# A layer of experts, attention and experts: constant products on TensorE and a new order of work in the routing stage

## The chip, the cores and the metric

The kernel runs on one core of one Trainium2 chip. The metric is the device time of one execution in microseconds (us): the median of the runs, and beside it one execution that the hardware profiler recorded. A core has five engines that run side by side and meet at semaphores: TensorE (PE: matrix products; PEld is its loading of weights), VectorE (DVE), ScalarE (ACT), GpSimd (POOL) and SyncE (SP), whose queue issues most DMAs.

## The reference

The input x is 2 x 2048 tokens of width 256, so 4096 tokens. Three layers follow each other, each with a layer norm before it and a residual sum behind it:

```
x = x + 0.5 * ffn(layernorm(x))     # router: 8 experts, the best 2 of each token; silu(gate) * up, down
x = x + attention(layernorm(x))     # causal convolution to q, k, v of width 64; 8 heads; blocks of 128 tokens
x = x + 0.5 * ffn(layernorm(x))     # the same experts again
```

In an ffn, `logits = h @ router_w.T`; the two largest probabilities of a token, normalised to sum 1, weigh the outputs of their experts (hidden width 176).

## The kernel before

Tokens lie in 32 tiles of 128. An expert layer doesn't run all experts on all tokens: it sorts the 8192 pairs of token and expert by expert into slots, in 71 tiles of 128 slots, gathers the rows of each slot tile, runs the one expert of that tile, and adds the two results of each token later. So three stages are long and regular: the experts of the first layer (from about 82 us to 231 us of the span), the attention with the routing of the last layer, and the experts of the last layer. The change touches the first stage, which ends when the first expert tile can start at about 82 us: it normalises all 32 tiles, computes router logits, finds each token's two experts and slots, and splits the experts' weights in two.

Every engine runs one list of instructions in a fixed, hand-written order. A wait at the head of a list holds all that is behind it. In the first stage the lists are:

- **SP**: loads of x in 8 chunks, then the experts' weights, then the stores of normalised rows of tile groups 0 and 1 (`stored0`, `stored1`), 13 small loads for the attention, then the stores of groups 2 and 3. A group is 8 tiles.
- **GpSimd**: a few constants, the correction of the reciprocal roots of two parts of the tiles (`correct_roots`, one Newton step in small operations), 16 or so further constants (`other_constants`), the roots of the other three parts, a first indirect DMA to warm up (`warm_up`, which it waits for), and then the gathers of rows (L655), which wait for the token table `tok_i`.
- **ScalarE**: logarithm and exponential for the roots (`seed`), the normalisation of tile t + 4 (`norm`, L866), the copy of the turned tile t out of PSUM (L882), and in the turns 22, 25, 28 and 30 the high parts of the weights of experts 0 to 3 (`weights`, L872). After the loop it evicts what TensorE makes of the low parts (`lows`, L894), with the high parts of experts 4 to 7 between, and some weights of the attention. Last comes an exponential (`difference`) and the load of the table for silu (L748).
- **TensorE**: in each turn of `first_router` two transposes of a tile (L1447) and the logits of the tile before (L1454: two f32 products of 8 columns, that the trace shows as four). `first_ranks(g)` (L1471 to L1477) counts, for a group, how many earlier tokens chose each expert. `low_parts(e)` (L1507, L1508) subtracts the high part of an expert's weights from the whole in PSUM, in three pieces; `first_counts` gives the totals; `first_table(g)` (L1491) turns the slots of a group into the table of tokens, from the lanes and the tile marks of the group.
- **VectorE**: means and variances (`first_stats`), `constants`, and for each group g: `first_pick(g)` (L1002 to L1017: the two experts), `first_places(g)` (L1026 to L1035: the slots, after the ranks), `first_lanes(g)` (L1041: 16 operations of 128x128 that mark the lane of each slot). After all groups come `first_starts` (L1055 to L1063), the tile marks `first_tiles` (L1048), the lanes of group 3, the low part of the last expert (`low_part`, L1068), the token table `tok_i` (L1105), and a few products for the attention and the weights of the sums.

The lanes of groups 2 and 3 lie over the buffer that holds the normalised rows of group 2 (the tensor `yg`), so VectorE waits for `stored2` before it writes the first of them. The order of the end is this:

```python
for g in range(GROUPS - 1):
    first_tiles(g)
first_lanes(3, 0, GROUP)
first_tiles(3)
...
for e in range(PE_LOW, E):
    low_part(e)
v.wait_ge(first["table"], 1)
```

Of the kernel before, what the change touches and what calls it, by code (L numbers as in the profile page):

```python
# [15 lines left out]
ALU = mybir.AluOpType  # L16
# [4 lines left out]
BF16 = mybir.dt.bfloat16  # L21
# [3 lines left out]
P = 128  # L25
# [4 lines left out]
E, TOPK = 8, 2  # L30
# [20 lines left out]
PROJB_AT = 5  # L51
HEAD_AT = [4 * (h % 2) + h // 2 for h in range(NH)]
GROUP = 8
GROUPS = TILES // GROUP
STATS = ((0, 4), (4, 4), (8, 8), (16, 8), (24, 8))
# [6 lines left out]
WEIGHTS_AFTER = {22: 0, 25: 1, 28: 2, 30: 3}  # L62
PE_LOW = 7
# [33 lines left out]
def macaron_kernel(nc, x, conv_w, conv_b, wq, wk, wvT, wo, bq, bk, bo, proj_w, proj_b, gupT, dpT, rwT,  # L97
                   out, h_dram, y_dram):
    ctx = ExitStack()
    with ctx:  # L100
# [149 lines left out]
        def lane_num(j):  # L250
            return lane_halves[j // TILES][:, j % TILES, :]
# [25 lines left out]
        mask_4 = mask_bf[:, :].unsqueeze(1).to_broadcast([P, 4, P])  # L277

# [299 lines left out]
        def _(pool):  # L578
# [127 lines left out]

            stats_of = list(enumerate(STATS))
            correct_roots(stats_of[0:2])
            other_constants()
            correct_roots(stats_of[2:])  # L710
            warm_up()
            gather_rows(0)
# [7 lines left out]
        def _(a):  # L720
# [42 lines left out]
            def attention():  # L763
# [77 lines left out]
                a.wait_ge(projb, 4)  # L841
# [11 lines left out]
            def first_norm():  # L853
# [26 lines left out]
                for t in range(TILES):  # L880
                    a.wait_ge(first["transposed"], t + 1)
                    a.activation(hT_sb[:, t % 2, :], (A, B)[t % 2][:, 0:D], ACT.Copy).then_inc(first["copied"], 1)  # L882
                    if t in SEED_AFTER:
                        seed(SEED_AFTER[t])
                    if there(t + LEAD):
                        norm(t + LEAD)
                    if t in WEIGHTS_AFTER:
                        weights(WEIGHTS_AFTER[t])

# [6 lines left out]
                for e in range(4):  # L896
                    lows(e)
                    weights(e + 4)
                a.wait_ge(loaded, 16 * len(loads))
                attention_weights()  # L900
                for e in range(4, PE_LOW):
                    lows(e)
# [29 lines left out]
        def _(v):  # L932
# [137 lines left out]
            def first_layer():  # L1070
                r = R[0]
                for c in range(4):
                    first_stats(c)
                constants()
                for c in range(4, len(STATS)):
                    first_stats(c)
                first_pick(0)
                first_places(0)
                first_pick(1)
                first_lanes(0, 0, GROUP)  # L1080
                first_places(1)
                first_lanes(1, 0, GROUP)
# [6 lines left out]
                v.tensor_tensor(wtmp[:, 1, :], best[:, :, 1], best[:, :, 0], ALU.subtract).then_inc(r["diff"], 1)  # L1089
                first_lanes(2, GROUP // 2, GROUP)  # L1090
                first_places(3)
# [10 lines left out]
                for e in range(PE_LOW, E):  # L1102
                    low_part(e)
# [3 lines left out]
                v.wait_ge(first["turned"], 1)  # L1107
                v.tensor_scalar(at_i[:, 0:TABLE_TILES], CC[0:1, EXPERTS_AT:EXPERTS_AT + TABLE_TILES], float(EW), None,
                                ALU.mult).then_inc(r["weights_at"], 1)
                v.wait_ge(wprep, 5)  # L1110
# [298 lines left out]
        def _(pe):  # L1409
# [29 lines left out]

            def first_router():  # L1440
                z = first

                def turn(t):
                    pe.wait_ge(z["normed"], t + 1)
                    pe.wait_ge(z["copied"], t + 1)
                    for c in range(DC):
                        i = pe.transpose((A, B)[t % 2][:, c * P:(c + 1) * P],  # L1447
                                         h_rings[t // GROUP][:, t % GROUP, c * P:(c + 1) * P], ident[:, :])
                    i.then_inc(z["transposed"], 1)

# [35 lines left out]
            def first_table(g):  # L1486
                n = GROUP * TOPK
                pe.wait_ge(first["lanes"], g + 1)
# [236 lines left out]

            pe.wait_ge(rw_in, 16)
# [5 lines left out]
            first_ranks(GROUPS - 1)  # L1732
            low_parts(2)
            first_counts()
            low_parts(3)
            pe.wait_ge(loaded, 16 * len(loads))
            weights_vo()
            low_parts(4)
# [3 lines left out]
            low_parts(5)  # L1742
            first_table(GROUPS - 1)
            turn_experts()
            low_parts(6)
# [5 lines left out]
            pe.wait_ge(projb, 3)  # L1751
            pe.wait_ge(qk_scaled, 2)
            pe.wait_ge(const, 5)
# [50 lines left out]
```

## Time and profile before

| | |
|---|---|
| median of 3 runs | 793.61 us (789.54 to 793.93) |
| the profiled execution's own time | 796.36 us |
| its span, first to last instruction | 794.6 us |
| busy in the span | PE 690.0, PEld 603.7, DVE 528.2, ACT 490.2, POOL 335.8 us |
| mean granted TensorE clock | 0.961 |

The span is that of the one profiled execution; 1.8 us of its own time lie around the span, and it is 2.7 us above the median of the runs. Times in rows of the timeline count from the start of the span. A row of the timeline is: start, duration, engine (with q for its queue of issued DMAs), line, operation, what it writes and reads, shapes, and in brackets the idle time before it and what ended that. xN merges N neighbours of the same kind, so the duration is that of all of them.

### The profile page before, as it was taken

How to read it: one execution, taken by the hardware profiler on the slowest of the kernel's cores; microseconds unless marked ns; L12 is line 12 of the kernel's file. 1: busy time of each engine (PE TensorE's matmuls, PEld its weight loads, DVE VectorE, ACT ScalarE, POOL GpSimd, SP SyncE). 2: the span in 40 equal slices, each digit the busy share in tenths (PEclk: the TensorE clock that was granted, in tenths of full speed). 3: DMA queues.
4: the chain of work that ended last, by engine and by line, in shares of the span. 5: the costliest groups of instructions: out<-in, count | busy, mean ns of one | idle time of the engine just before them, and what ended most of it. 6: DMA issues, size and time to landing. Idle time of an engine off the chain costs nothing. (4 is left out here: it accounts for less than half of the span.)

```text
span 794.6 us, 19426 instructions
## 1 busy us (share of the span) xinstructions
PE 690.0 (87%) x5468; PEld 603.7 (76%) x5468; DVE 528.2 (66%) x1813; ACT 490.2 (62%) x1734; POOL 335.8 (42%) x361
## 2 busy tenths in 40 slices
PE   3999799999999799998988889989635999999944
PEld 3976699999975688877767777778424999999833
DVE  6578566666656587786767576857664777777643
ACT  4766566666653587767766657767522666666633
POOL 5100544444416444455555545252551444444500
PEclk9999999999999999999999999999956999999979
DMA  9930354444422110011111111010124444444279
GB/s 313 279 110 13 124 147 141 143 130 127 128 82 85 39 41 28 28 41 55 55 55 48 61 41 48 22 55 2 61 91 117 132 128 125 128 131 126 83 288 346
DMA packets 57863, 83.40 MB, mean 105 GB/s; under 512 B 9520, under 2 KB 43827, under 8 KB 57780
## 3 DMA queue, kind: packets, MB, share of 16 engines
q1 hardware_dynamic: 44772, 47.63, 19.0%
q0 software_dynamic: 13008, 34.69, 14.0%
q8 instruction: 49, 0.80, 0.4%
q14 instruction: 34, 0.28, 0.1%
HBM read 45.77 MB, written 37.44 MB: 105 GB/s over the span
## 5 line engine op out<-in xcount | busy, mean ns | idle before, releaser
L1539 PE MATMUL CC<-w_hi,turned_parts 128*128 x568 | 172.5, 345 | 0.3 <-DVE turned_parts L1161 0.2
L655 POOL DMA_INDIRECT shared<-h_rows,tok_i x71 | 67.3, 948 | 119.0 <-issue 58.7
L667 POOL DMA_INDIRECT y_rows<-shared,y_dest x71 | 69.9, 985 | 88.7 <-DVE y_dest L1173 74.9
L683 POOL TENSOR_TENSOR pr<-pr,prec 128x1024 f32<-128x1024 f32 x31 | 58.8, 1895 | 112.2 <-DVE prec L1353 110.9
L1539 PEld LDWEIGHTS CC<-w_hi,turned_parts 128*128 128x128 f32 x568 | 103.8, 190 | 1.0 <-issue 0.9
L1539 PE MATMUL CC<-w_lo,turned_parts 128*128 x284 | 91.8, 323 | 0.0
L729 ACT ACTIVATE shared<-CC 128x176 f32<-128x176 f32 x142 | 45.1, 317 | 75.1 <-PE CC L1539 72.6
L813 ACT ACTIVATE pr<-SS,nmax 128x128 f32<-128x128 f32 x256 | 90.4, 400 | 0.8 <-issue 0.8
L700 POOL DMA_INDIRECT h_regions<-h_store,dest x64 | 63.1, 987 | 47.3 <-DVE dest L1256 27.3
L1156 DVE TENSOR_TENSOR shared<-shared,CC 128x176 f32<-128x176 f32 x142 | 48.0, 338 | 51.6 <-ACT shared L729 30.0
L691 POOL DMA_INDIRECT yg<-y_rows,slot_i x64 | 62.6, 977 | 34.9 <-DMA y_rows<-shared 15.5
L745 ACT ACTIVATE shared<-SS 128x256 f32<-128x256 f32 x142 | 54.6, 385 | 26.5 <-issue 15.5
L804 ACT ACTIVATE shared<-CC 128x512 f32<-128x512 f32 x64 | 34.7, 594 | 48.1 <-PE CC L1629 45.2
L813 ACT ACTIVATION_READ_ACCUMULATOR pr<-SS,nmax 128x1 f32 x256 | 61.8, 241 | 0.0
L1539 PEld LDWEIGHTS CC<-w_lo,turned_parts 128*128 128x128 f32 x284 | 54.1, 191 | 0.0
L1556 PE MATMUL SS<-w_hi,turned_parts 128*128 x142 | 51.8, 364 | 1.3 <-DVE turned_parts L1167 1.0
L1161 DVE TENSOR_TENSOR turned_parts<-A,turned_parts 128x256 fp32r<-128x256 f32 x72 | 30.6, 425 | 29.5 <-ACT turned_parts L734 28.5
L1311 DVE TENSOR_REDUCE nmax<-SS 128x8 f32<-128x1024 f32 x32 | 39.1, 1221 | 13.4 <-PE SS L1623 10.4
L1623 PEld LDWEIGHTS SS<-shared 64*128 64x128 f32 x512 | 31.1, 187 | 18.0 <-issue 9.7
L1161 DVE TENSOR_TENSOR turned_parts<-B,turned_parts 128x256 fp32r<-128x256 f32 x70 | 29.8, 425 | 21.0 <-ACT turned_parts L734 16.8
L1526 PE MATMUL A<-ident,shared 128*128 128x128 f32 x144 | 29.0, 283 | 16.1 <-DMA shared<-h_regions 12.6
L781 ACT ACTIVATE lnvar<-moments,eps 128x2 f32<-128x2 f32 x39 | 11.7, 300 | 48.9 <-DVE moments L1367 48.0
(318 smaller groups left out, 2055.4 us busy)
## 6 DMA issues: line engine op xcount, KB each, us to landing
shared<-h_regions SPq DMA_DIRECT2D x71, 129.0 KB
y_rows<-shared SPq DMA_DIRECT2D x71, 128.0 KB
w_lo<-y_rows SPq DMA_DIRECT2D x9, 512.0 KB, 8.4
x_sb<-in_x_dram SPq DMA_DIRECT2D x8, 512.0 KB, 8.3
out_dram<-x_sb SPq DMA_DIRECT2D x16, 256.0 KB, 5.7
w_hi<-y_rows SPq DMA_DIRECT2D x7, 512.0 KB, 11.9
w_lo<-in_gupT_dram SPq DMA_DIRECT2D x2, 1408.0 KB, 10.7
h_regions<-pad_rows SPq DMA_DIRECT2D x15, 129.0 KB
```

The source lines that it names most:

```text
L655: pool.indirect_dma_start(out=rows[:, s % RING, 0:D], out_offset=None, in_=h_dram[:, :], in_offset=bass.IndirectOffsetOnAxis(ap=tok_i[:, s ...
L667: pool.indirect_dma_start(out=y_dram[0:TOPK * TOKENS, :], out_offset=bass.IndirectOffsetOnAxis(ap=y_dest[:, s:s + 1], axis=0), in_=y_sb[:, ...
L683: pool.tensor_tensor(pr[:, q, :, :], pr[:, q, :, :], prec[:, q, :].unsqueeze(2).to_broadcast([P, NH, P]), ALU.mult).then_inc(t["norm"], 1)
L691: pool.indirect_dma_start(out=yg[:, q, k, :], out_offset=None, in_=y_dram[:, :], in_offset=bass.IndirectOffsetOnAxis(ap=slot_i[:, b, k:k + ...
L700: pool.indirect_dma_start(out=h_regions[:, :], out_offset=bass.IndirectOffsetOnAxis(ap=dest[:, q, k:k + 1], axis=0), in_=hr[:, q, :], in_o ...
L729: a.activation(gate[:, p, :], CC[:, 512 * p:512 * p + H], ACT.Silu).then_inc(r["silu"], 1)
L745: a.activation(y_sb[:, u % RING, :], SS[:, 512 * (u % 2):512 * (u % 2) + D], ACT.Copy).then_inc(r["y_sb"], 1)
L813: e = a.activation(pr[:, u % 2, h, :], SS[:, h * P:(h + 1) * P], ACT.Exp, bias=nmax[:, u % 2, h:h + 1], accum_out=psums[:, u % 2, h:h + 1])
L1156: v.tensor_tensor(hid[:, p, 0:H], gate[:, p, :], CC[:, 512 * p + H:512 * p + GU], ALU.mult).then_inc(r["hid"], 1)
L1161: v.tensor_tensor(rowsT_lo[:, p, :], (A, B)[p][:, 0:D], rowsT_hi[:, p, :].bitcast(F32), ALU.subtract).then_inc(r["rowsT_lo"], 1)
L1539: i = pe.matmul(CC[:, 512 * (u % 2):512 * (u % 2) + GU], rows_part[:, u % 2, c * P:(c + 1) * P], weights, start=(n == 1), stop=(n == 3 * DC))
L1556: pe.matmul(acc, hidA_hi[:, u % 2, :], w_hi[:, at_a], start=True, stop=False)
```

## The change

All edits lie in the first stage.

- **Constant products.** VectorE clears a bf16 tile of 128x128 (`idle_bf`, over the buffer `rank4`, which is free then) as its first instruction. TensorE waits for it and then runs 28 products of 512 columns with it into PSUM bank CC, before it waits for the router weights. After the two transposes of every turn it runs one more such product. Nothing reads the results.
- **Roots and statistics.** VectorE makes all five parts of the statistics before `constants`. GpSimd corrects the roots of three parts, not two, before its further constants.
- **Lanes.** GpSimd makes the lanes of groups 0 and 1, 16 operations each, after its warm-up DMA and before it waits for the stores and `tok_i`; VectorE tells it on the semaphore `const` when the places of a group are there. VectorE keeps groups 2 and 3.
- **Order on VectorE.** The second half of the lanes of group 2 comes after `first_places(3)` instead of before. One more expert's low part is VectorE's (`PE_LOW` is 6, not 7: TensorE and ScalarE make experts 0 to 5, VectorE 6 and 7), and both come after `tok_i` instead of before.
- **Order on ScalarE.** No weights in the turns; after the loop `weights(0)`, `weights(1)`, and then for e of 0 to 5 `lows(e)` and `weights(e + 2)`, with the attention's weights after e = 2.
- **Order on TensorE.** `first_counts` follows the ranks of group 3 at once; the attention's products come after `low_parts(2)`, and each later piece of the list is one `low_parts` earlier.

```diff
-PROJB_AT = 5
+PROJB_AT = 6
...
-WEIGHTS_AFTER = {22: 0, 25: 1, 28: 2, 30: 3}
-PE_LOW = 7
+PE_LOW = 6
...
+        idle_bf = rank4[:, :, :, :].rearrange("p i k e -> p (i k e)").bitcast(BF16)
...
+            def first_lanes(g):
+
+                pool.wait_ge(const, 5 + g)
+                for b in range(g * GROUP, (g + 1) * GROUP):
+                    for k in range(TOPK):
+                        ins = pool.tensor_scalar(lane_num(TOPK * b + k), iota_h[:, :], slane[:, b, k:k + 1],
+                                                 number_off[:, b:b + 1], ALU.is_equal, ALU.mult)
+                ins.then_inc(first["turned"], 1)
+
             stats_of = list(enumerate(STATS))
-            correct_roots(stats_of[0:2])
+            correct_roots(stats_of[0:3])
             other_constants()
-            correct_roots(stats_of[2:])
+            correct_roots(stats_of[3:])
             warm_up()
+            first_lanes(0)
+            first_lanes(1)
             gather_rows(0)
...
-                    if t in WEIGHTS_AFTER:
-                        weights(WEIGHTS_AFTER[t])
...
-                for e in range(4):
+                weights(0)
+                weights(1)
+                for e in range(PE_LOW):
                     lows(e)
-                    weights(e + 4)
-                a.wait_ge(loaded, 16 * len(loads))
-                attention_weights()
-                for e in range(4, PE_LOW):
-                    lows(e)
+                    weights(e + 2)
+                    if e == 2:
+                        a.wait_ge(loaded, 16 * len(loads))
+                        attention_weights()
...
-                for c in range(4):
+                v.memset(idle_bf[:, :], 0.0).then_inc(projb, 1)
+                for c in range(len(STATS)):
                     first_stats(c)
                 constants()
-                for c in range(4, len(STATS)):
-                    first_stats(c)
                 first_pick(0)
                 first_places(0)
+                v.sem_inc(const, 1)
                 first_pick(1)
-                first_lanes(0, 0, GROUP)
                 first_places(1)
-                first_lanes(1, 0, GROUP)
+                v.sem_inc(const, 1)
...
+                first_places(3)
                 first_lanes(2, GROUP // 2, GROUP)
-                first_places(3)
                 first_starts()
...
-                for e in range(PE_LOW, E):
-                    low_part(e)
                 v.wait_ge(first["table"], 1)
...
-                v.wait_ge(first["turned"], 1)
+                v.wait_ge(first["turned"], 3)
...
+                for e in range(PE_LOW, E):
+                    low_part(e)
                 v.wait_ge(wprep, 5)
...
+            def busy_clock(n):
+
+                for _ in range(n):
+                    pe.matmul(CC[:, 0:512], idle_bf[:, :], idle_bf[:, :].unsqueeze(1).to_broadcast([P, 4, P]),
+                              start=True, stop=True, skip_group_check=True)
+
...
                     i.then_inc(z["transposed"], 1)
+                    busy_clock(1)
...
-                pe.wait_ge(first["lanes"], g + 1)
+                if g < 2:
+                    pe.wait_ge(first["turned"], g + 1)
+                else:
+                    pe.wait_ge(first["lanes"], g - 1)
...
+            pe.wait_ge(projb, 1)
+            busy_clock(28)
             pe.wait_ge(rw_in, 16)
             pe.wait_ge(made, 3)
             first_router()
...
             first_ranks(GROUPS - 1)
+            first_counts()
             low_parts(2)
-            first_counts()
-            low_parts(3)
             pe.wait_ge(loaded, 16 * len(loads))
             weights_vo()
-            low_parts(4)
+            low_parts(3)
             bias_vo()
             for g in range(GROUPS - 1):
                 first_table(g)
-            low_parts(5)
+            low_parts(4)
             first_table(GROUPS - 1)
             turn_experts()
-            low_parts(6)
+            low_parts(5)
```

The remaining edits shift counts of the semaphores `projb` and `const` by what is added to them.

## Rows read from the trace of the kernel before

**Rows 1.** Timeline of GpSimd (POOL) in the first stage.

```profile
13.95 0.29 POOL L599 CAST ident_bf<-ident 128x128 bf16<-128x128 f32 x1
...
31.97 1.19 POOL L639 DMA_INDIRECT shared<-in_x_dram,part_i  x1 [0.17 <-issue]
...
78.01 0.97 POOL L655 DMA_INDIRECT shared<-h_rows,tok_i  x1 [44.85 <-DVE tok_i L1105]
```

**Rows 2.** Timeline of TensorE (PE) in the first stage.

```profile
16.01 0.67 PE L1447 MATMUL A<-ident,h_store 128*128 128x128 f32 x2
...
24.03 0.67 PE L1447 MATMUL A<-ident,pr 128*128 128x128 f32 x2
...
25.21 0.67 PE L1447 MATMUL B<-ident,pr 128*128 128x128 f32 x2
...
52.53 1.95 PE L1507 MATMUL A<-w_lo,ident 128*128 128x480 f32 x2
...
57.63 1.04 PE L1507 MATMUL B<-w_lo,ident 128*128 128x480 f32 x2
...
60.50 0.20 PE L1471 MATMUL CC<-sel_bf,before_bf 128*128 128x64 bf16 x1
...
75.95 0.69 PE L1491 MATMUL CC<-tile_oh,yg 128*128 128x72 f16 x16
...
81.54 0.44 PE L1526 MATMUL A<-ident,shared 128*128 128x128 f32 x2 [1.89 <-DMA shared<-h_rows,tok_i]
```

**Rows 3.** Timeline of ScalarE (ACT) in the first stage.

```profile
25.91 0.38 ACT L882 ACTIVATE hT_sb<-B 128x256 f32<-128x256 f32 x1 [0.30 <-PE B L1447]
...
58.04 1.30 ACT L872 ACTIVATE w_hi<-w_lo 128x960 fp32r<-128x960 f32 x2
...
80.20 1.28 ACT L748 ACT_TABLE_LOAD   x1
```

**Rows 4.** Timeline of VectorE (DVE) in the first stage.

```profile
31.72 0.27 DVE L1026 TENSOR_REDUCE group_sum<-sel_bf 128x8 f32<-128x64 bf16 x1 [5.48 <-PE CC L1477]
...
36.73 3.66 DVE L1041 TENSOR_SCALAR shared<-iota_h,slane,number_off 128x128 f16<-128x128 f16 x16 [0.15 <-DVE sel_bf L1017]
...
63.73 0.17 DVE L1055 COPY ecnt<-CC 128x8 f32<-128x8 f32 x1 [1.19 <-PE CC L1483]
...
66.61 3.90 DVE L1048 TENSOR_TENSOR tile_oh<-iota_h,stile_h 128x1152 f16<-128x1152 f16 x3 [0.18 <-DVE stile_h L1063]
...
73.99 1.35 DVE L1048 TENSOR_TENSOR tile_oh<-iota_h,stile_h 128x1152 f16<-128x1152 f16 x1
...
75.59 1.48 DVE L1068 TENSOR_TENSOR w_lo<-w_lo,w_hi 128x960 fp32r<-128x960 f32 x2
76.99 0.22 DVE L1105 TENSOR_SCALAR tok_i<-CC 128x72 int32<-128x72 f32 x1
...
77.27 0.67 DVE L1111 TENSOR_TENSOR wvo_lo<-SS,wvo_hi 128x512 fp32r<-128x512 f32 x1
...
80.22 0.18 DVE L1119 TENSOR_SCALAR wtmp<-wtmp 128x32 f32<-128x32 f32 x1 [2.08 <-ACT wtmp L919]
...
82.50 0.42 DVE L1161 TENSOR_TENSOR turned_parts<-A,turned_parts 128x256 fp32r<-128x256 f32 x1 [0.75 <-ACT turned_parts L734]
```

**Rows 5.** Timeline of the queue of SyncE: the store of group 2.

```profile
40.12 0.40 SPq L498 DMA_DIRECT2D h_rows<-yg  x1
```

**Rows 6.** DMA issues of the first 84 us: name, count, size, median us to landing.

```profile
h_rows<-yg SPq DMA_DIRECT2D x1, 1024.0 KB, 4.4
```

**Rows 7.** Timeline of TensorE: constant products ahead of the attention.

```profile
233.02 9.67 PE L1581 MATMUL F<-mask_bf,ident_bf 128*128 128x512 bf16 x44
```

**Rows 8.** Windows of 5 us: busy time of each engine, granted clock (PEclk), DMA share, GB/s.

```profile
20.00:25.00 5.00, 5.00 (x28) 5.00 (x28) 2.77 (x23) 4.00 (x12) 1.26 (x6) 1.00 1.08 289
...
85.00:90.00 5.00, 2.80 (x19) 2.25 (x19) 1.99 (x8) 1.54 (x7) 2.14 (x3) 1.00 0.22 64
...
260.00:265.00 5.00, 2.48 (x8) 2.22 (x9) 3.01 (x7) 3.30 (x18) 0.94 (x1) 0.71 0.18 54
265.00:270.00 5.00, 4.74 (x42) 3.91 (x41) 4.10 (x10) 1.47 (x4) 3.84 (x3) 0.94 0.11 31
```

More of the change, by code:

```diff
@@ L840, in attention @@
                 a.activation(projb_all[:, D:], zeros[:, 0:G_USED - D], ACT.Copy)
-                a.wait_ge(projb, 4)
+                a.wait_ge(projb, 5)
                 a.activation(projb_all[:, 0:D], G[:, 0:D], ACT.Copy).then_inc(projb, 1)
@@ L1750, in _ @@
             experts(R[0])
-            pe.wait_ge(projb, 3)
+            pe.wait_ge(projb, 4)
             pe.wait_ge(qk_scaled, 2)
-            pe.wait_ge(const, 5)
+            pe.wait_ge(const, 7)
             pe.matmul(G[:, 0:D], ones_r[:, :], projb_parts[:, :], start=True, stop=True).then_inc(projb, 1)
```

## Prediction

> **What bounds the kernel now.** All edits lie ahead of the first expert tile, so I first looked for what decides when that tile starts, in the timelines of the engines, from the end backwards. TensorE turns the first gathered rows at 81.54 us, after waiting for their DMA [rows 2]. GpSimd issued that gather at 78.01, after 44.85 us of waiting for `tok_i` [rows 1]. VectorE wrote `tok_i` at 76.99, and ahead of it worked without a pause: tile marks, lanes, tile marks, a low part [rows 4]. So VectorE's list behind the router loop sets the start. ScalarE comes close: its table load ends at 81.48 [rows 3], just as the rows arrive. The start of that list is set by the loop on TensorE: a turn takes 1.18 us (24.03 to 25.21), the loop ends at 52.53 where `low_parts` begins [rows 2], and ScalarE waits for TensorE inside it (0.30 us before a copy) [rows 3].
>
> The reader should also see at which clock the loop runs. The granted clock of 20 to 25 us reads 1.00 [rows 8], but the rows of the work say the lower level (1.2 GHz): the same pair of f32 products of 480 columns takes 1.95 us at 52.53 and 1.04 us at 57.63 [rows 2]. I take the column to be empty ahead of its first event. TensorE rose behind five us of dense products, and the loop before, of transposes and products of 8 columns, had not raised it.
>
> Everything behind the start (experts, attention, experts) is untouched. I take it to shift as a whole, so the result is the move of that start.
>
> **The loop.** Removed from ScalarE's turns: the high parts of four experts, 1.2 us each without the overlap of the rows' 1.30 [rows 3]; they move behind the loop, where ScalarE otherwise waits for TensorE. Added: one product of 512 columns per turn. At the upper level (2.4 GHz) it takes 9.67 / 44 = 0.22 us [rows 7], at the lower twice that, 0.44. If the clock is high, a turn is half of 1.18 plus 0.22 = 0.81 us; some latencies don't halve, so 0.81 to 0.86. If it is low, 1.18 + 0.44 = 1.62, or 1.45 where weight loads hide under the product. Turn 4 starts at 16.01 before [rows 2]; up to there the loop hangs on the first roots, which don't move, so I place it at 15.1 with fast transposes. The third part of the roots comes ahead of GpSimd's constants, so turns 5 to 10, which took 8.0 us instead of 6 x 1.18 = 7.1 (16.01 to 24.03) [rows 2], no longer pause. GpSimd's constants move behind it, and VectorE's first pick waits for them until about 21.5 us; its ranks are wanted after turn 15, so that is covered. With 27 turns of 0.83 (22.4), three rank groups and two pairs of seeds (1.5), and 0.5 for a wait on the picks of group 1, turn 31 runs at 39.5 to 40.1. The ranks and places of group 2 then end at about 42.3.
>
> **The 28 products.** They start at about 1.1 us, run at the lower level first, and end between 9 and 10.5, by when in the run the clock rises. Turn 0 hangs on the first roots until about 9.8, and ScalarE can't copy its result until about 11.4. So they cost nothing, up to about 1 us more than the cover.
>
> **VectorE's list.** Its next wait is `stored2`: SP issued that store at 40.12 behind 13 loads [rows 5], and it took 4.4 us to land [rows 6], so 44.5. The loads themselves are behind x and the weights, where the DMA engines are full, so an earlier `stored1` frees at most 1.5 us: 43.0 to 44.5, and I take 43.5. This new wait hides about 1 us of the loop. From there the rows of before can be added: half the lanes of group 2, 1.8; pick and places of group 3, 5.0 (31.72 to 36.73, the same pair for other groups); the other half, 1.8; starts, 2.9 (63.73 to 66.61); three tile marks, 3.9; lanes of group 3, 3.6; last marks, 1.3 [rows 4]. That is 20.3, so the marks end at 63.8. TensorE has been waiting, and its table of group 3 takes 0.7 [rows 2]; `tok_i` starts at 65.0, not 76.99. That is 12.0 us earlier. Of these the loop gives about 8 to 9, the 32 lanes that leave VectorE 2 x 3.66 (partly in waits before), and the low part of 1.5 behind `tok_i` the last piece.
>
> **What is late next.** Two low parts are now behind `tok_i`, and the last high part is behind `lows(5)`. TensorE starts `low_parts(5)` behind the table, at 65.0, and takes 2.9 us (57.63 to 60.50) [rows 2]: 67.9. ScalarE evicts (0.4) and makes the high part of expert 7, 1.2 [rows 3]: 69.5. VectorE's second piece of its low part ends at 70.5, `wvo_lo` adds 0.7 [rows 4], and TensorE may start at about 71.3. ScalarE, with exponential and table load 1.3 [rows 3], is ready at 70.9. The rows landed at 65.9 + 3.5 = 69.4 (78.01 to 81.54 before). VectorE still has the weights of the sums (from 80.22 to its first low rows at 82.50 it took 2.3, with 0.75 of waiting, so 1.5) and starts its first expert work at 73.0, not 82.50 [rows 4]. The move of the start is 9.5 us: 2.5 of the 12.0 go to this tail.
>
> **Lanes on GpSimd.** No row has this operation there. The nearest is a cast of 128x128 at 0.29 us [rows 1]; I take 0.35, with 0.25 and 0.8 as bounds. GpSimd is free after its warm-up DMA, which was issued at 31.97 [rows 1] and comes some 5 us earlier; it waits for the landing, so the lanes start at about 33.5 and end at 44.7, or 59.1 at 0.8. They are wanted at about 59.2, with the tile marks of group 2. So the price can be anything up to 0.8 at no cost; from there each 0.1 adds 3.2 us. Behind them on GpSimd stand only the gathers, which wait for `tok_i` anyway. For the two engines in each other's way I add 0.5 us. The sum is -9.0 us: 787.4 on the profiled execution's own 796.36, and 784.6 on the median, which is 2.7 below it. Less than nothing isn't excluded for the lanes: VectorE may gain from a calmer list, but `stored2` caps it, at 1 us.
>
> **Rival 1: the clock stays low, slower.** Between turn 0 and turn 4 TensorE waits for roots and copies, and does little. In a stretch without any work the clock fell (0.71 in 260 to 265) and came back only with dense products (0.94 in the next) [rows 8]. If it falls there and one product of 512 columns a turn can't raise it, turns take 1.45 to 1.62 instead of 0.83: turn 31 runs at 56 to 60, VectorE's list starts 14 to 18 us later than 43.5, and the sum is +5 to +9: 801 us. For it speaks the old loop, which never rose; against it that with gaps and 2.8 busy us of 5 the clock stayed up from 85 to 90 [rows 8], and that a product of 512 columns is a large part of a turn. The point of decision is whether the loop runs high from about turn 6 on. The Trainium skill ("TensorE: Matmul & The Clock Gate", Part 4) says that transposes don't count as work for the clock in the way products do. By that rule the transposes of the loop help nothing and the constant products must carry it alone; the old loop agrees, but no row here tells its share of products from its share of transposes. A fall that is made good by turn 6 or 8 costs 0 to 3 us, of which `stored2` hides 1.
>
> **Rival 2: GpSimd and VectorE block each other.** If each of VectorE's operations that meets a lane waits for it, and each lane for one of VectorE's (0.25), a lane takes 0.6 and the lanes end at 52.7. From 43.5 to 52.7 some 15 operations of VectorE wait 0.35 each: +5, so 790 us. In the rows of before, small operations of GpSimd ran beside statistics without a visible delay, but that is one input on VectorE. The Trainium skill ("SBUF — State Buffer", section "SBUF: two separate sides") states such an exclusive lock on a shared pair of ports, for two-input and fast modes of VectorE. It is a rule against this change, and no row of before has such a pair side by side.
>
> **Rival 3: the wait is only moved.** If `stored2` lands no earlier than 44.5 and the tail is 1 us longer (last high part), the sum is -7: 786.6.
>
> **How the numbers follow.** One per cent is 7.9 us, about what a measurement of this kernel can tell from no change. The forecast (high clock, -7 to -11.5) has 0.55, with its own range of 782 to 787; rival 1 has 0.2, rival 2 0.1, rival 3 or a late return of the clock 0.1, and other things 0.05. Faster by over 1% needs at least -7.9: three quarters of the forecast's cases, and some larger gains, 0.5. Slower by over 1% is half of rival 1 and some others, 0.14. The rest, 0.36, is within 1%. The range runs from 780.5, with `stored2` at 43.0 and no conflict, to 800.5, which takes in rivals 2 and 3 and the better edge of rival 1.
>
> **What would show it.** Pairs of transposes in the loop start 0.8 to 0.9 us apart (else 1.45 to 1.6); turn 31 near 40; a wait of VectorE for the store before its first lanes; `tok_i` near 65.0; lanes on GpSimd of 0.35 us; the first low rows at about 73.0. The prediction is wrong if the clock is low in the loop, if a lane costs over 0.8, or if the last weights hold the experts longer than 2.5 us.

## The result, and the profile after

The changed kernel took 801.73 us (median of 4 runs, 799.1 to 803.79), the kernel before 792.25 in the same comparison: a ratio of 1.0118, with an interval of 1.0085 to 1.0151. It is slower by 9.5 us, where I forecast 784.6 us, 9.0 less than the median on record then. What happened is rival 1: the clock falls in the head and stays low through the loop.

The windows of the changed kernel show it first. The column after POOL is the granted clock; the row of 20 to 25 us answers to the first of [rows 8].

```profile
5.00:10.00 5.00, 3.77 (x18) 1.51 (x16) 4.69 (x21) 1.26 (x4) 1.86 (x9) 1.00 1.06 347
10.00:15.00 5.00, 2.91 (x17) 2.08 (x18) 4.71 (x23) 3.68 (x11) 1.44 (x7) 0.94 1.11 351
15.00:20.00 5.00, 5.00 (x23) 4.54 (x24) 3.78 (x24) 3.36 (x9) 3.36 (x17) 0.50 1.04 381
20.00:25.00 5.00, 5.00 (x23) 4.54 (x23) 1.34 (x11) 2.98 (x8) 0.97 (x6) 0.50 1.09 269
...
60.00:65.00 5.00, 5.00 (x26) 3.92 (x27) 1.99 (x10) 2.78 (x5) 5.00 (x8) 0.50 0.00 0
```

The 28 products bring the clock up (they take 7.71 us below, 0.28 each, where the lower level would give 0.44); between 10 and 15 us TensorE has 2.91 us of work, and from 14.37 us on the granted clock is 0.50, that is 1.2 GHz, until 68.98. The row of 15 to 20 us is the instructive one: TensorE is shown busy for all of it, and so it is in the turns behind it, and yet the clock is not granted again. The timeline of TensorE (start, duration, line, operation) shows the two levels of the clock and the path to the first expert tile:

```profile
1.06 7.71 PE L1453 MATMUL CC<-rank 128*128 128x512 bf16 x28 [1.06 <-DVE rank L1083]
...
12.80 0.38 PE L1453 MATMUL CC<-rank 128*128 128x512 bf16 x1
14.24 0.94 PE L1471 MATMUL F<-rw_sb,hT_sb 128*128 128x8 f32 x4 [1.06 <-ACT hT_sb L894]
15.04 0.67 PE L1463 MATMUL B<-ident,h_store 128*128 128x128 f32 x2
15.49 0.63 PE L1453 MATMUL CC<-rank 128*128 128x512 bf16 x1
...
60.45 0.67 PE L1463 MATMUL B<-ident,tile_oh 128*128 128x128 f32 x2
...
63.21 1.95 PE L1527 MATMUL A<-w_lo,ident 128*128 128x480 f32 x2
...
87.39 0.68 PE L1511 MATMUL CC<-tile_oh,yg 128*128 128x72 f16 x16 [1.48 <-DVE tile_oh L1059]
...
95.32 0.41 PE L1546 MATMUL A<-ident,shared 128*128 128x128 f32 x2 [4.24 <-DVE mha_bias L1122]
```

The product at 12.80 takes 0.38 us, the one at 15.49 takes 0.63; the transposes go from 0.41 to 0.67, which is what they took before [rows 2]. Turns are now 1.60 us apart, against 1.18 before: the added product costs its full 0.42 us in each. Turn 31 runs at 60.45, and the first expert's rows are turned at 95.32, not at 81.54 [rows 2]. VectorE and GpSimd answer to [rows 4] and [rows 1]:

```profile
62.69 0.27 DVE L1037 TENSOR_REDUCE group_sum<-sel_bf 128x8 f32<-128x64 bf16 x1 [8.44 <-PE CC L1494]
...
88.11 0.23 DVE L1113 TENSOR_SCALAR tok_i<-CC 128x72 int32<-128x72 f32 x1 [0.55 <-PE CC L1511]
...
92.43 1.53 DVE L1079 TENSOR_TENSOR w_lo<-w_lo,w_hi 128x960 fp32r<-128x960 f32 x2 [2.48 <-ACT w_hi L884]
...
96.26 0.42 DVE L1171 TENSOR_TENSOR turned_parts<-A,turned_parts 128x256 fp32r<-128x256 f32 x1
```

```profile
40.48 25.23 POOL L713 TENSOR_SCALAR shared<-iota_h,slane,number_off 128x128 f16<-128x128 f16 x32 [3.39 <-DMA shared<-in_x_dram,part_i]
...
89.15 1.72 POOL L656 DMA_INDIRECT shared<-h_rows,tok_i  x1 [23.45 <-DVE tok_i L1113]
```

VectorE waits 8.44 us for the ranks of group 2, so the loop, not VectorE's list, holds the start. A lane table on GpSimd takes 25.23 / 32 = 0.79 us, not 0.35, but ends at 65.7, before anyone wants it. From `tok_i` (88.11) to TensorE's first rows (95.32) it is 7.2 us instead of 4.6: the wait ends on `mha_bias`, behind the last low part, behind ScalarE's last high part.

### The profile page after: what moved, and what is told of

Its sections match the earlier page's. It is cut to its first block, busy times and chain, and to the rows that moved or that the text cites. A ratio compares the mean times of both kernels' runs of the same rounds, so it can differ in the third digit from the quotient of the medians.

```text
span 801.7 us, 19528 instructions
## 1 busy us (share of the span) xinstructions
PE 703.1 (88%) x5519; PEld 611.1 (76%) x5519; DVE 524.0 (65%) x1784; ACT 491.7 (61%) x1731; POOL 362.0 (45%) x393
## 3 DMA queue, kind: packets, MB, share of 16 engines
q0 software_dynamic: 13008, 34.69, 13.8%
## 4 chain that ended last, share of the span: by engine, by line
PE 77%; issue 7%; DVE 6%; DMA 4%; ACT 3%; SPq 2%; another core or an unknown queue 1%; POOL 1%; DVEq 0%; POOLq 0%; ACTq 0%
PE CC L1559 17%; PE CC L1709 4%; PE SS L1643 4%; PE CC L1649 4%; PE B L1622 4%; PE F L1699 4%; PE F L1719 3%; PE B L1631 3%; PE A L1546 3%; PE SS L1576 2%; PE SS L1577 2%; PE SS L1578 2%; PE SS L1579 2%; PE SS L1580 2%; PE B L1546 2%
## 5 line engine op out<-in xcount | busy, mean ns | idle before, releaser
L701 POOL DMA_INDIRECT h_regions<-h_store,dest x64 | 63.5, 992 | 43.4 <-issue 21.9
L1576 PE MATMUL SS<-w_hi,turned_parts 128*128 x142 | 51.7, 364 | 1.0 <-DVE turned_parts L1177 0.7
```

Of the source, the lines that this page charges most:

```text
L701: pool.indirect_dma_start(out=h_regions[:, :], out_offset=bass.IndirectOffsetOnAxis(ap=dest[:, q, k:k + 1], axis=0), in_=hr[:, q, :], in_o ...
L1576: pe.matmul(acc, hidA_hi[:, u % 2, :], w_hi[:, at_a], start=True, stop=False)
```

## The experiments

All ratios are to the kernel before on the same chip in the same comparison. The chips differ: the kernel before took 757.9 us (median of 19) beside e1 to e4, 792.7 (27) beside e5 to e8, 758.8 (20) beside e9 to e12. So only ratios and the times of the first stage are compared across groups; for the changed kernel, the one that was profiled on two chips, its start agrees within 1.4 us. "Start" is the time at which TensorE turns the first gathered rows; it was 81.54 before [rows 2].

**e1: the changed kernel without any constant product.**

```diff
-                    busy_clock(1)
...
-            busy_clock(28)
```

> The changed kernel without any constant product (neither the 28 nor the one per turn); all else as changed. Theory A (the clock falls between turn 1 and turn 4, and one product of 512 columns a turn costs 0.43 us at the lower level and doesn't raise it again): turns start 1.18 us apart instead of 1.60, turn 31 at about 49 instead of 60.45, the first expert tile about 11.5 us earlier than in the changed kernel, time about 790 us. Theory B (the lanes on GpSimd, 0.79 us each instead of 0.35, and their clash with VectorE are what costs): the time stays near 800. Theory C (the tail behind tok_i, 7.2 us from tok_i to the first expert tile instead of 4.5, is the whole loss): then at least 799, since the tail is unchanged here.

Measured: 759.03 us (10 runs), ratio 1.0020, interval 1.0005 to 1.0035. The loop and the work behind it, on TensorE:

```profile
47.62 0.67 PE L1463 MATMUL A<-ident,tile_oh 128*128 128x128 f32 x2
...
48.79 0.67 PE L1463 MATMUL B<-ident,tile_oh 128*128 128x128 f32 x2
...
83.42 0.41 PE L1545 MATMUL A<-ident,shared 128*128 128x128 f32 x2 [4.24 <-DVE mha_bias L1122]
```

Turns are back at 1.17 us, and nearly all of the loss is gone: the products cost it. But the rest of the change isn't worth the 3 us or so that was expected of it. The loop ends 1.4 us earlier than before (48.79 against 50.19), `tok_i` comes 0.8 earlier (76.21 against 76.99), and the longer tail, 7.2 us, takes more than that back: the start is 1.9 us later. With 32 lanes off VectorE its last marks still end at 75.34, as before (73.99 + 1.35 [rows 4]): those lanes lay in waits for the loop.

**e2: the changed kernel with more products in turns 1 to 5, where the head was sparse.**

```diff
+HEAD_FILL = {1: 5, 2: 6, 3: 2, 4: 2, 5: 2}
...
-                    busy_clock(1)
+                    busy_clock(HEAD_FILL.get(t, 1))
```

> The changed kernel with more constant products in the sparse head of the loop: 5 after turn 1, 6 after turn 2, 2 after each of turns 3 to 5, and one after all others as now; they fill waits of TensorE. Theory A: the clock doesn't fall at 14 us, stays at 2.4 GHz through the loop with one product a turn, turns start 0.83 to 0.86 us apart, turn 31 at about 40, tok_i near 65 to 66, the first expert tile near 72 to 73, time 780 to 784 us. The lanes then end at about 59, just when the table wants them, and may cost up to 2 us more. Rival D (one product a turn can't hold the clock either): the clock falls later in the loop, turns go back to 1.60, time 790 to 803.

Measured: 754.29 us (10 runs), ratio 0.9955, interval 0.9929 to 0.9980. TensorE, then VectorE and GpSimd:

```profile
14.16 0.61 PE L1472 MATMUL F<-rw_sb,hT_sb 128*128 128x8 f32 x4
14.63 0.42 PE L1464 MATMUL B<-ident,h_store 128*128 128x128 f32 x2
...
20.26 0.42 PE L1464 MATMUL B<-ident,pr 128*128 128x128 f32 x2
...
63.92 0.69 PE L1512 MATMUL CC<-tile_oh,shared 128*128 128x72 f16 x16 [2.02 <-POOL shared L714]
64.45 0.69 PE L1512 MATMUL CC<-tile_oh,yg 128*128 128x72 f16 x16
64.97 1.62 PE L1528 MATMUL A<-w_lo,ident 128*128 128x480 f32 x2
...
69.32 0.70 PE L1512 MATMUL CC<-tile_oh,yg 128*128 128x72 f16 x16
...
77.22 0.66 PE L1547 MATMUL A<-ident,shared 128*128 128x128 f32 x2 [4.20 <-DVE mha_bias L1123]
```

```profile
44.44 2.20 DVE L1053 TENSOR_SCALAR yg<-iota_h,slane,number_off 128x128 f16<-128x128 f16 x8 [1.32 <-DMA h_rows<-yg]
...
57.65 3.89 DVE L1060 TENSOR_TENSOR tile_oh<-iota_h,stile_h 128x1152 f16<-128x1152 f16 x3 [0.18 <-DVE stile_h L1075]
...
65.04 1.34 DVE L1060 TENSOR_TENSOR tile_oh<-iota_h,stile_h 128x1152 f16<-128x1152 f16 x1
...
70.06 0.23 DVE L1114 TENSOR_SCALAR tok_i<-CC 128x72 int32<-128x72 f32 x1 [3.34 <-PE CC L1512]
```

```profile
33.82 30.05 POOL L714 TENSOR_SCALAR shared<-iota_h,slane,number_off 128x128 f16<-128x128 f16 x32 [4.62 <-DVEq L1093]
```

The merged row of GpSimd holds one lane that differs from all others. The same timeline asked for 58 to 61 us shows it alone:

```profile
57.69 4.38 POOL L714 TENSOR_SCALAR shared<-iota_h,slane,number_off 128x128 f16<-128x128 f16 x1
```

The transposes keep their 0.42 us, turns are 0.83 us apart, turn 31 runs at 40.19: with the head filled, this is the very loop that I forecast. One product a turn keeps the clock to the end of the loop; it first falls at 51.7 us. Yet the gain is 3.4 us, not 9. Three things take it. VectorE first waits for the store of group 2. GpSimd's tables end only at 63.87, and TensorE waits 2.02 us for them: of its 32 lanes 31 take 0.8 us in the mean, and one takes 4.38, from 57.69 to 62.07. That one begins 0.04 us behind the first of VectorE's three tile marks (57.65 to 61.54) and ends 0.5 behind the last of them, while the marks take no longer than before (3.89 against 3.90 [rows 4]). At 0.79 us for it GpSimd would have been done at about 60.3 (an estimate: 63.87 less 3.6), ahead of TensorE's first table at 61.21. And the clock, having fallen at 65.3, makes the low parts between the tables slow (1.62 us instead of 1.04), so that VectorE waits 3.34 us for its table.

**e3: the kernel before with the products alone (28 and one a turn).**

```diff
+                    busy_clock(1)
...
+            busy_clock(28)
```

> The kernel before with the constant products alone (28 ahead, one per turn), no other edit. Theory A: the clock falls in the head as in the changed kernel, turns start 1.60 apart, turn 31 8 to 9 us later than 50.19, time 799 to 802. If the fall is due to the new order, the clock holds here and the time is 783 to 788.

Measured: 768.97 us (4 runs), ratio 1.0153, interval 1.0122 to 1.0184. Granted clock 0.50 from 16.2 to 67.4 us, turns of 1.60, turn 31 at 59.57, start at 91.55. The loss needs nothing but the products: they alone move the start by 10.0 us of the 13.8 in the changed kernel. The other parts don't cure it, and e1's longer tail is a further 1.9 of the move.

**e4: the kernel before with the products and the filled head of e2.**

> The kernel before with the filled head of e2 (28 ahead; 5, 6, 2, 2, 2 after turns 1 to 5, one after all others), no other edit. Theory A: the clock holds, turn 31 near 44, VectorE's own lanes of groups 0 and 1 come between picks and places and take part of it back, tok_i near 70, time about 785. Rival D: near 800.

Measured: four runs of two kinds, 750.83 and 752.97 us at a granted clock of 0.962 and 0.960, and 764.77 and 767.52 at 0.938 and 0.933. No ratio of the whole says anything here; the two runs of the first kind lie 0.8% below the kernel before (751.9 against 757.9). The profiled run is of the first kind, with turns of 0.83, turn 31 at 44.15 and the start at 73.91. It also shows where TensorE was left without work. The roots come in the old order, so ScalarE's normalisation of a later tile waits 2.09 us for them, and the copy that the logits want stands behind it:

```profile
18.03 0.38 PE L1447 MATMUL CC<-rank 128*128 128x512 bf16 x1
19.85 0.61 PE L1465 MATMUL F<-rw_sb,hT_sb 128*128 128x8 f32 x4 [1.44 <-ACT hT_sb L885]
```

The profiled run kept its clock through this gap (1.00 from 15 to 70 us), and no run of the second kind was profiled.

**e8: e4 with six more products in turn 6, in that gap.**

```diff
-HEAD_FILL = {1: 5, 2: 6, 3: 2, 4: 2, 5: 2}
+HEAD_FILL = {1: 5, 2: 6, 3: 2, 4: 2, 5: 2, 6: 6}
```

> The kernel before with the filled head (e4) and six more constant products at turn 6, where the roots of tiles 8 to 15 were late (1.44 us of idle TensorE). Theory A (a gap in the head lets the clock fall, and one product a turn does not raise it): the two kinds of runs of e4 (granted clock about 0.96 and 0.935) become one kind at about 0.96, ratio about 0.991. Rival (the split is made somewhere else, behind the loop): the granted clock differs between runs as in e4 and the median ratio is near 1.0.

Measured: 784.86 us (6 runs, 781.9 to 787.5), ratio 0.9911, interval 0.9876 to 0.9945; granted clock 0.942 to 0.959, all runs of one kind. The gap is 0.34 us now:

```profile
18.04 1.46 PE L1447 MATMUL CC<-rank 128*128 128x512 bf16 x6
19.83 0.61 PE L1465 MATMUL F<-rw_sb,hT_sb 128*128 128x8 f32 x4 [0.34 <-ACT hT_sb L885]
```

With e4 this is what theory A wanted, but not more than that: e4's four runs and e8's six are of different chips, and e6, whose head is filled too, goes down to 0.936 on e8's chip. e8 also has the lowest ratio of the first eight kernels, with an interval that overlaps those of e2, e5, e6 and e7, and it holds nothing of the change but the products: roots, high parts, counts and lanes are those of the kernel before. Its loop ends 3.9 us after e2's (44.12), and its `tok_i` comes at 69.24, ahead of e2's 70.06.

**e5: e2 with the lane tables of groups 0 and 1 back on VectorE.**

```diff
-            first_lanes(0)
-            first_lanes(1)
...
                 first_pick(1)
+                first_lanes(0, 0, GROUP)
                 first_places(1)
+                first_lanes(1, 0, GROUP)
...
```

> The changed kernel with the filled head of e2, and the lane tables of groups 0 and 1 back on VectorE, behind the first roots and places. Theory B (GpSimd's tables, 0.94 us each to 63.87, are waited for 2.02 us at the end and the clock falls in the waits that follow): VectorE carries 16 more short instructions but nothing waits for GpSimd; the ranks end at the right time, tok_i lands near 66.9 instead of 70.1, the first expert's work near 74.0 instead of 77.2, the ratio to the kernel before about 0.991 (e2: 0.9955). Rival (VectorE's own list is as late as GpSimd's): tok_i at 69.5 to 70.5 and a ratio of 0.995 to 0.996.

Measured: 786.63 us (10 runs), ratio 0.9939, interval 0.9912 to 0.9966. VectorE:

```profile
46.00 1.88 DVE L1051 TENSOR_SCALAR yg<-iota_h,slane,number_off 128x128 f16<-128x128 f16 x8 [0.18 <-DVE slane L1045]
...
66.98 1.34 DVE L1058 TENSOR_TENSOR tile_oh<-iota_h,stile_h 128x1152 f16<-128x1152 f16 x1
...
69.19 0.23 DVE L1113 TENSOR_SCALAR tok_i<-CC 128x72 int32<-128x72 f32 x1 [0.53 <-PE CC L1508]
```

`tok_i` at 69.19 lies between theory (66.9) and rival. The wait for GpSimd is gone, and the marks follow on each other, but they end at 68.3, not 66.4 as in e2: VectorE has the 32 lanes (7.3 us) on its own list again. With GpSimd's lanes the start was 77.22, without them it is 76.36, less than 1 us apart; e2's blocked lane is in the first of the two.

**e6: e5 with the high parts of experts 5, 6 and 7 all behind the low parts of expert 3 on ScalarE.**

> e5 with ScalarE's high parts of experts 5, 6 and 7 all issued behind the last low part of the head. Theory C (the tail from tok_i to the first expert is 7.2 us instead of 4.5 because the last high part and, behind it, the low parts on VectorE are late): tail 4.7 to 5.0 us, first expert's work near 71.7, ratio about 0.988. Rival (the tail waits for the clock or the rows, not for the parts): tail stays at 7 us and the time is e5's within 1 us.

Measured: 788.41 us (10 runs, 780.78 to 792.12), ratio 0.9944, interval 0.9908 to 0.9981. VectorE and TensorE:

```profile
68.21 2.87 DVE L1080 TENSOR_TENSOR w_lo<-w_lo,w_hi 128x960 fp32r<-128x960 f32 x4
...
71.02 0.67 DVE L1123 TENSOR_TENSOR wvo_lo<-SS,wvo_hi 128x512 fp32r<-128x512 f32 x1
```

```profile
73.72 0.44 PE L1545 MATMUL A<-ident,shared 128*128 128x128 f32 x2 [2.90 <-DMA shared<-h_rows,tok_i]
```

The low parts run without the 2.5 us wait, the tail is 5.9 us instead of 7.2, and its end is the landing of the rows, no longer the weights. Theory C is right on the cause and 1 us short on the price, because the rows then bind. The start is 2.6 us earlier than e5's, but the time isn't: the ten runs go from 780.8 us at a granted clock of 0.961 to 792.1 at 0.938. Its profiled run has short falls of the clock at 225, 256, 379 and 461 us; but e8's has four as well (253, 376, 396, 512) and lost nothing by them, and e5's has two (255, 480). What spreads e6's runs stays open.

**e7: the changed kernel with two products in each turn.**

```diff
-                    busy_clock(1)
+                    busy_clock(2)
```

> The changed kernel with two constant products in each turn instead of one, head not filled. If one product a turn is too little to raise the clock and two are enough: granted clock falls near 14 to 16 us, turns of about 2.0 us at the lower level, then it is raised again and the turns take about 1.05 us; turn 31 between 42 and 55, ratio between 0.995 and 1.012. Rival (two don't raise it either): all turns at about 2.0 us, turn 31 near 72, ratio 1.02 to 1.03.

Measured: 788.75 us (10 runs), ratio 0.9945, interval 0.9913 to 0.9977. Neither guess: the clock doesn't fall at all in the head.

```profile
13.95 0.61 PE L1471 MATMUL F<-rw_sb,hT_sb 128*128 128x8 f32 x4 [0.84 <-ACT hT_sb L894]
14.42 0.41 PE L1463 MATMUL B<-ident,h_store 128*128 128x128 f32 x2
14.67 0.59 PE L1453 MATMUL CC<-rank 128*128 128x512 bf16 x2
```

Turns take 1.05 us, turn 31 runs at 44.47, the start at 78.03. One more product a turn makes the whole difference between 1.012 and 0.9945; in the window from 10 to 15 us TensorE had 3.88 us of work instead of 2.91. As the clock never fell, whether two products a turn can raise it again wasn't seen.

**e9: e6 with the lanes of group 0 alone on GpSimd.**

> e6 with the lane tables of group 0 alone on GpSimd. Theory D (the list of VectorE sets the end of the marks once the clock is held; GpSimd is worth what it takes off that list, as long as it is not waited for): 16 lanes of 0.23 us (3.7 us) leave VectorE, GpSimd is done with its 16 near 48, other VectorE instructions run slower beside it by 0.5 to 1.5 us in all; tok_i near 65.5 (e6: 67.85), first expert's work near 71.5, ratio about 2 us, 0.0025, below e6's 0.9944. Rival (the two engines hold each other up by as much as is taken off): tok_i at 67.5 to 68.5, ratio equal to e6's.

Measured: 750.32 us (5 runs), ratio 0.9903, interval 0.9871 to 0.9935, the lowest ratio measured. But `tok_i` came at 68.42, not 65.5:

```profile
45.73 2.07 DVE L1054 TENSOR_SCALAR yg<-iota_h,slane,number_off 128x128 f16<-128x128 f16 x8 [2.35 <-DMA h_rows<-yg]
...
68.42 0.23 DVE L1115 TENSOR_SCALAR tok_i<-CC 128x72 int32<-128x72 f32 x1 [1.54 <-PE CC L1513]
```

The 3.7 us taken off VectorE's list turn into 2.35 us of waiting for the store and, at the end, 1.54 for TensorE. SyncE issued that store at 41.02 and it had landed by 45.7. Theory D falls as stated: the list alone doesn't set the end; with the loop at 0.83 us the store is just as late. `tok_i` is where the rival had it (67.5 to 68.5), but most of the gain goes into these two waits, not into the two engines' being in each other's way. On the start (74.39 against e6's 73.72) this edit gains nothing, so the better ratio than e6's isn't shown to be its doing.

**e10: the changed kernel again, on the chip of e9 to e12.**

> The changed kernel itself once more, on the chip of the other runs of this call. Expected as measured first: clock at the lower level from about 14 to 69 us, ratio 1.009 to 1.015. Rival: on another chip the head keeps its clock and the ratio is near 0.995.

Measured: 770.80 us (4 runs), ratio 1.0171, interval 1.0145 to 1.0196. Granted clock 0.50 from 14.6 to 65.8 us, turns of 1.60, start at 93.95. The fall is no accident of a chip.

**e11: e8 with the lanes of group 0 on GpSimd.**

> e8 (the kernel before with constant products and filled gaps) with the lane tables of group 0 on GpSimd. Theory D: tok_i 1.5 to 3 us ahead of e8's 69.24, first expert's work near 72, ratio about 0.988. Rival: no gain over e8 (0.9911).

Measured: 757.00 us (10 runs, 749.9 at a granted clock of 0.968 to 759.2 at 0.944), ratio 0.9969, interval 0.9939 to 0.9998. `tok_i` at 69.44, start at 74.15, as in e8. VectorE waits 3.21 us for the ranks of group 2 in place of the lanes. A second miss of theory D.

**e12: the kernel before with 28 products and two in each turn.**

> The kernel before with the 28 constant products and two in each turn, no gap filled specially. If two a turn hold the clock whatever the order of the roots: turns of 1.05 us, a wait of about 1 us at turn 6, turn 31 near 49, tok_i near 70, ratio 0.991 to 0.995. Rival (the gap at turn 6 lets the clock fall): some runs or all at a granted clock of 0.93 and a ratio near 1.0 to 1.01.

Measured: 755.02 us (10 runs); ratio 0.9954, interval 0.9926 to 0.9982, from eight of them. Turns of 1.05, turn 31 at 46.54, start at 76.25. These eight lie between 752.5 and 759.9, the other two at 767.0 and 770.2 with a granted clock of 0.942 and 0.939. That would fit a gap at turn 6 that sometimes costs the clock, as in e4, but it isn't shown: neither of the two was profiled, and the profiled run kept its clock through a gap of 1.20 us there.

**The start and the time.** The move of the start against 81.54, divided by the time before, beside the measured change:

| kernel | start, us | move | as a share | measured |
|---|---|---|---|---|
| changed | 95.32 | +13.8 | +1.7% | +1.2% |
| e1 | 83.42 | +1.9 | +0.2% | +0.2% |
| e2 | 77.22 | -4.3 | -0.6% | -0.45% |
| e3 | 91.55 | +10.0 | +1.3% | +1.5% |
| e5 | 76.36 | -5.2 | -0.65% | -0.6% |
| e6 | 73.72 | -7.8 | -1.0% | -0.6% |
| e7 | 78.03 | -3.5 | -0.4% | -0.55% |
| e8 | 74.31 | -7.2 | -0.9% | -0.9% |
| e9 | 74.39 | -7.2 | -0.9% | -1.0% |
| e10 | 93.95 | +12.4 | +1.6% | +1.7% |
| e11 | 74.15 | -7.4 | -1.0% | -0.3% |
| e12 | 76.25 | -5.3 | -0.7% | -0.45% |

The start explains the time within 0.25% for all but three: the changed kernel as first measured, of which more below, and e6 and e11, whose runs spread with the granted clock. e4 is left out; its start was 73.91.

## Why the prediction was wrong

**The step that failed: the clock in the loop.** The forecast took turns of 0.81 to 0.86 us at the upper level; rival 1 had them at 1.45 to 1.62, turn 31 at 56 to 60, 801 us. Measured: 1.60, 60.45, 801.73. The mechanism was on paper and had too small a chance. I held two things against it: that the clock had stayed up from 85 to 90 us with gaps [rows 8], and that a product of 512 columns is a large part of a turn. The first row was of another kind of work, the experts' products; the second was an argument without a row. The only rows that resembled the loop were the loop's own, 37 us long, which never rose [rows 2], and those I had read rightly. e2, e4 with e8, and e7 show the cause from both sides: fill the gaps of the head, or double the products, and the clock stays; leave them and it is gone by 14 to 16 us and does not return in 45 us of turns with one product each. Filling a gap and adding work are one edit here, so no run says which of the two holds it. By the Trainium skill ("TensorE: Matmul & The Clock Gate", Part 4) the transposes don't count as work for the clock in the way products do; by that rule the change was weaker than its busy time looks. The trace is consistent with it: the turns from 15 us on are 5.00 of 5 us busy and the clock is at 0.50. But no run has other work in the place of the transposes, so the rule isn't tested here.

**Rival 1's own sum was too small on the path.** I priced the later start at +5 to +9 us. In the trace the start moved by 13.8. The late end of that range has VectorE's list begin at 61.5 and take 20.3 us; it began at 64.52, since the last ranks and places run at the lower clock too, and took 22.7, to the end of the last marks at 87.24. In e10 the start moved by 12.4, and there the time moved by as much (0.0171 x 758.8 = 13.0). On the first chip it moved by 9.5 only, and so rival 1's 801 us came close to 801.73 partly by luck. In that chip's two profiled runs the stage from the first experts' end to the second's start took 374.7 us in the changed kernel and 380.1 in the kernel before, which had two short falls of the clock in it (mean 0.83 and 0.74 in these windows) where the changed kernel had 1.00 from 440 to 450:

```profile
440.00:450.00 10.00, 8.50 (x65) 7.26 (x64) 5.64 (x15) 6.02 (x24) 5.04 (x5) 0.83 0.18 54
...
468.00:473.00 5.00, 3.77 (x21) 3.25 (x22) 4.02 (x14) 3.83 (x17) 2.49 (x2) 0.74 0.00 0
```

Whether that is chance of single executions or a habit of that chip isn't settled. "Everything behind the start shifts as a whole" holds to about 0.25% for nine of the twelve kernels of the table.

**With the clock held, the sum would still have been wrong.** e2 is the forecast's own case. First low rows were forecast at 73.0 and came at 78.41, 5.4 us later. By terms:

- The loop: 39.5 to 40.1 forecast for turn 31, 40.19 measured, 0.1 off. The price of a turn, 0.83, was right.
- The store of group 2: 43.5 forecast, 44.44 measured, +0.9. In e9, with nothing else in the way, VectorE got past it at 45.7.
- VectorE's list: 20.3 forecast, 21.9 measured (44.44 to 66.38), +1.6. Most is in pick and places of group 3: 6.2 us instead of 5.0, 0.7 of it a wait for the ranks. The 16 lanes of group 2 beside GpSimd took 4.2 instead of the forecast's 3.6.
- From the last marks to `tok_i`: 1.2 forecast, 3.7 measured, +2.5. This is the term that I didn't have: the tables of groups 0 and 1, for which I asked only whether GpSimd is done before VectorE's marks, stand in TensorE's queue ahead of low parts, which stand ahead of the last table. A lane cost GpSimd 0.79 where I took 0.35, just inside the bound of 0.8, and by itself that would have been in time; the one lane of 4.38 was not. A fall of the clock came on top, in the low part behind the wait.
- The tail: 8.0 forecast, 8.35 measured. Right; e6 confirms what it hangs on.

**The parts.** The 28 products cost nothing, as forecast: turn 0 starts at 10.11 with them and at 10.33 without (e1), and they end at 8.8, a little before the 9 to 10.5 forecast. The third part of the roots ahead of the constants does what I said: turns 4 to 10 run without the pause that e3 and e4 still have at turn 6. But with the clock held that gain isn't visible in the start. **Rival 2** had the mechanism of e2's late tables, with another victim. Only a few operations of VectorE got longer beside lanes (at 42.88 in e1 one took 0.56 instead of 0.29), but one lane of GpSimd waited for VectorE, 3.6 us over its 0.79, beside three tile marks in a row that read two tensors each. The Trainium skill ("SBUF — State Buffer", section "SBUF: two separate sides") has an exclusive lock for VectorE's fast modes, and for its instructions with two inputs in SBUF against a GpSimd operation that reads SBUF. The trace of e2 agrees: 4.38 us beside the marks. It is the only lane that met one: in the changed kernel, e1, e7, e9, e10 and e11 the lanes end before the first tile mark begins, and none takes over 0.97 us. That is also why rival 2 costs nothing in the changed kernel (lanes to 65.70, marks from 78.51). With short operations the two engines disturb each other less: VectorE's 8 lanes take 2.20 us beside GpSimd's in e2 and 1.88 alone in e5. **Rival 3** isn't separated from the rest.

## What to carry to other kernels

In this kernel one constant product a turn held a granted clock and didn't regain a lost one; 28 in a row did raise it at the start. Put them where TensorE would otherwise be idle between its last dense work and the loop, and look for the granted clock of the very turns, not of similar work elsewhere: with the same product a turn got 0.35 us shorter with the clock held (1.18 to 0.83) and 0.42 longer without. When a loop gets shorter by 10 us, price every list that ran in its shadow. Here VectorE's list, a store and the last weight parts were each within 1 to 3 us of becoming the end, so that undoing or moving one of them (e5, e9, e11) moved the start by less than 1 us. When a row merges many operations, look at the longest one too: a mean of 0.94 us hid 31 lanes of 0.8 and one of 4.38. And the simplest edit did as well as any: the kernel before, products only, gaps filled, at 0.9911 (0.9876 to 0.9945). No difference to e9 (0.9903, 0.9871 to 0.9935), which keeps most of the change, is shown.

## What the runs showed that I had not expected

- One product of 512 columns a turn keeps the clock up when it is up (e2: the turns from the sixth on, 0.83 us each, at 1.00) and doesn't bring it back when it is down (28 turns of 1.60 us at 0.50 in the changed kernel, with TensorE busy 5.00 of 5 us). The products of 480 columns behind the loop brought it back each time (after: they start at 63.21, and the clock is 1.00 from 68.98 on; before: [rows 2]).
- A gap of 1.44 us at turn 6 in e4 went with two kinds of runs, 14 us apart; with 0.34 us of gap (e8, on another chip) there was one kind. That the gap is the cause isn't shown.
- Three two-input operations of VectorE in a row held up one operation of GpSimd from start to end: 4.38 us instead of 0.79 (e2), with no slowing of VectorE's own (3.89 against 3.90).
- A lane table of 128x128 in f16 with two per-partition operands costs GpSimd 0.79 us and VectorE 0.23, less than a third. The first is 2.7 times GpSimd's cast of the same tile, 0.29 [rows 1], which I took as the nearest row.
- The kernel before takes 757.9 and 758.8 us on two chips and 792.7 on a third; in the runs that were profiled the difference lies between the two expert stages (341 to 345 us against 375 to 380); the first stage of the changed kernel agrees within 1.4 us (start at 95.32 and 93.95).
